# Gated cross-attention kernel: in the transfer queue, queries and keys are written and read back before the probabilities are written

## The reference

```python
def _L1_xattn_ref(hidden_states, cross_attention_states, attention_mask, Wq, Wk, Wv, Wo, q_norm_w, k_norm_w):
    q = (hidden_states @ Wq.T).reshape(bsz, q_len, H, HD).transpose(0, 2, 1, 3)
    k = (cross_attention_states @ Wk.T).reshape(bsz, kv_len, KVH, HD).transpose(0, 2, 1, 3)
    v = (cross_attention_states @ Wv.T).reshape(bsz, kv_len, KVH, HD).transpose(0, 2, 1, 3)
    q = _rmsnorm(q, q_norm_w)
    k = _rmsnorm(jnp.repeat(k, GROUPS, axis=1), k_norm_w)
    scores = jnp.einsum('bhqd,bhkd->bhqk', q, k) * scale + attention_mask[:, :, :, :kv_len]
    probs = jax.nn.softmax(scores.astype(jnp.float32), axis=-1).astype(q.dtype)
    out = jnp.einsum('bhqk,bhkd->bhqd', probs, v)
    return out.transpose(0, 2, 1, 3).reshape(bsz, q_len, H * HD) @ Wo.T
...
x = x + jnp.tanh(g_xattn[0]) * _L0_xattn_ref(_layernorm(x), ctx, ctx)
x = x + jnp.tanh(g_ffn[0]) * _L0_ffn_ref(_layernorm(x), ...)
x = x + jnp.tanh(g_xattn[1]) * _L1_xattn_ref(_layernorm(x), ctx, mask, ...)
x = x + jnp.tanh(g_ffn[1]) * _L1_ffn_ref(_layernorm(x), ...)
```

## Time and profile before

| | |
|---|---|
| runs, median of 3 | 743.99 us (740.37 to 744.77) |
| profiled execution, its own time | 738.72 us |
| its span in the trace | 736.9 us |
| PE busy | 712.1 us (97%) |
| DVE busy | 566.4 us (77%) |
| ACT busy | 377.6 us (51%) |
| POOL busy | 371.8 us (50%) |
| mean granted clock of TensorE | 0.995 |
| DMA | 110.31 MB, mean 150 GB/s |

### The profile page before, as it was taken

The page is one execution under the profiler, slowest core; times in us unless marked ns, Lnnn a source line. Parts: engine busy times, 40 slices in busy tenths (PEclk is TensorE's granted clock), DMA queues, the critical chain, the costliest instruction groups (busy, mean ns, idle before and its releaser), DMA issues.

```text
span 736.9 us, 12666 instructions
## 1 busy us (share of the span) xinstructions
PE 712.1 (97%) x3684; PEld 573.4 (78%) x3684; DVE 566.4 (77%) x1171; ACT 377.6 (51%) x1094; POOL 371.8 (50%) x429
## 2 busy tenths in 40 slices
PE   8899999988999999999999999999999999998996
PEld 5455556577888888888888888888888888887774
DVE  4888887566788777777877787787778787778784
ACT  5567664355555545544564545465545654454220
POOL 2568866556444634553564346345625642265331
PEclk9999999999999999999999999999999999999999
DMA  8400104145765675666657665756665666446221
GB/s 307 144 29 30 43 16 158 42 132 147 228 172 156 180 218 141 180 194 182 167 162 215 161 174 143 235 148 186 194 179 149 167 188 200 119 124 161 67 90 63
DMA packets 109283, 110.31 MB, mean 150 GB/s; under 512 B 12576, under 2 KB 78240, under 8 KB 108960
## 3 DMA queue, kind: packets, MB, share of 16 engines
q1 hardware_dynamic: 109216, 109.51, 52.6%
HBM read 69.62 MB, written 39.85 MB: 149 GB/s over the span
## 4 chain that ended last, share of the span: by engine, by line
PE 30%; POOL 21%; issue 16%; DMA 13%; DVE 11%; ACT 5%; SPq 4%; DVEq 0%; ACTq 0%; POOLq 0%
DMA pTf<-p_scratch 7%; POOL qkr L617 6%; POOL wo_lo L604 6%; PE pair L959 5%; PE pair L961 5%; PE pair L960 5%; DMA p_scratch<-p_blocks 4%; DVE qkn L1434 4%; SPq L458 3%; PE pair L999 3%; POOL wq_lo L596 2%; POOL prob L609 2%; PE pair L973 2%; POOL wkv_lo L586 2%; DVE p_blocks L1409 1%
## 5 line engine op out<-in xcount | busy, mean ns | idle before, releaser
L805 ACT ACTIVATE prob<-score,nmax 128x128 f32<-128x128 f32 x256 | 99.8, 391 | 147.8 <-DVE nmax L1399 147.8
L609 POOL TENSOR_TENSOR prob<-prob,erec 128x512 f32<-128x512 f32 x64 | 66.7, 1042 | 123.0 <-DVE erec L1419 123.0
L959 PE MATMUL pair<-wo_hi,oT_hi 128*128 128x512 f32 x256 | 107.3, 419 | 1.2 <-POOL wo_lo L604 1.2
L959 PE MATMUL pair<-wq_hi,nT_hi 128*128 128x512 f32 x256 | 101.7, 397 | 1.3 <-DVE qkn L1434 1.3
L960 PE MATMUL pair<-wo_lo,oT_hi 128*128 128x512 f32 x256 | 100.1, 391 | 0.0
L960 PE MATMUL pair<-wq_lo,nT_hi 128*128 128x512 f32 x256 | 100.0, 391 | 0.0
L961 PE MATMUL pair<-wo_hi,oT_lo 128*128 128x512 f32 x256 | 100.0, 391 | 0.0
L961 PE MATMUL pair<-wq_hi,nT_lo 128*128 128x512 f32 x256 | 100.0, 390 | 0.0
L1424 DVE TENSOR_REDUCE qkss<-qksq 128x5 f32<-128x640 f32 x64 | 52.4, 819 | 48.5 <-ACT qksq L812 48.2
L617 POOL TENSOR_TENSOR qkr<-qkse,neghalf 128x5 f32<-128x5 f32 x64 | 76.7, 1198 | 5.3
L812 ACT ACTIVATE qksq<-pair 128x640 f32<-128x640 f32 x64 | 45.0, 703 | 65.7 <-PE pair L961 65.7
(11 more groups left out here) (171 smaller groups left out, 1700.8 us busy)
## 6 DMA issues: line engine op xcount, KB each, us to landing
qk_scratch<-qk_blocks SPq DMA_DIRECT2D x256, 80.0 KB, 1.9
qkT<-qk_scratch SPq DMA_DIRECT2D x64, 320.0 KB, 3.0
p_scratch<-p_blocks SPq DMA_DIRECT2D x256, 64.0 KB, 1.8
pTf<-p_scratch SPq DMA_DIRECT2D x64, 256.0 KB, 3.4
wq_raw<-in_wq SPq DMA_DIRECT2D x32, 256.0 KB, 4.1
wo_raw<-in_wo SPq DMA_DIRECT2D x32, 256.0 KB, 4.8
wkv_raw<-in_wkv SPq DMA_DIRECT2D x8, 512.0 KB, 4.9
ctxn<-in_ctx_n SPq DMA_DIRECT2D x8, 256.0 KB, 3.3
```

Of the source, the lines that this page charges most:

```text
L609: pool.tensor_tensor(prob[:], prob[:], erec[:].unsqueeze(2).broadcast_to([P, BL, P]), ALU.mult).then_inc(normed, 1)
L805: t = act.activation(prob[:, i, :], score[:, i, :], ACT.Exp, bias=nmax[:, i:i + 1], accum_out=esum[:, i:i + 1])
L959: pe.matmul(out, l_hi, r_hi, start=start, stop=False)
```

## The change

In SP's loop the read of queries and keys of tile n+1 is issued directly behind their writes, in every slot, ahead of the writes of the probabilities of n-1; before, that was so in slots 0 and 1 alone. Nothing else differs.

```diff
                     if on(n + 1):
                         write_qk(n + 1)
-                    if n < 2 and on(n + 1):
                         read_qk(n + 1)
                     if on(n - 1):
                         write_probs(n - 1)
-                    if n >= 2 and on(n + 1):
-                        read_qk(n + 1)
-                    if on(n - 1):
                         read_probs(n - 1)
```

## The result

The change makes the kernel slower: 807.22 us median (804.05 to 808.54, 4 runs) against 743.98 (740.37 to 744.77, 4 runs), a ratio of 1.085 with a 95% interval of 1.081 to 1.090. The forecast was 748, and 740 to 759 as its range. The profiled execution's span is 805.7 us against 736.9. Its busy times hardly differ: DVE 564.2 us, ACT 374.9, POOL 371.3. PE's reads 729.2 us against 712.1, for the same 3684 products, with ends that are modelled.

What follows compares the result with a forecast made beforehand. TensorE was taken to bound the loop at 8.47 us a slot; +5.6 us behind weight loads and -1.6 at the end gave +4.0 on the median 743.99, so 748 us, range 740 to 759.

Steps and rivals of the forecast that it cites:

- TensorE bounds the loop before, and an edit to SP can only cost there: Attention loop: TensorE waits 1.2 us in 440, slots take 8.47 us, so an SP edit gains nothing there.
- A clean slot: Slot without weight loads: probabilities' read 2.2 us later, tile 1.2 us later, absorbed by ACT's 1.93 us idle; no cost.
- L: Landing time in an SP slot, from first write of queries and keys to their read-back; 3.17 us bare.
- L behind the four loads, taken at 4.5: Worst slot: landing between 3.17 and 5.51 us, about 1.0 less without 256 KB of probabilities; ACT's margin 0.3 us.
- L behind the other loads, taken at 3.9: Next slots, with one weight load each: landing assumed between 3.17 and 4.5 us.
- 3.78 for the probabilities' landing in every slot: Probabilities' first write to their read, from SP slot 1: 3.78 us, 0.56 more than the old order's 3.22.
- The lag, taken at 0.8 us a group: TensorE's loss behind weight loads in seven groups of eight slots: 5.6 us in all, bounds 0 and 16.
- the 2.3 us that I gave for landings of 5.51 and then 4.5: TensorE's loss a group behind weight loads if landings stayed as long as today's: about 2.3 us.
- Case 2, SP becomes the bound: Rival: SP's cycle in loading slots 9.17 us against 8.47, lag 18 us in all, about 760 us; chance 0.26.
- Lp: Time in an SP slot from the probabilities' first write to their read; the forecast used 3.78 us.
- The end of the loop: Last slots: earlier read-back shortens ACT's 3.90 us wait for keys; -1.6 us, bounds -1.0 and -3.2.
- The rule of the Trainium skill: SP queue: fixed transfer cost some 2 us, mostly last write's receipt, speaking against two waits in a row; sum unchanged.

Runs made afterwards that it cites:

- quiet_slots: Kernel before with the new order in SP slots with b = 0 and 1 alone (16 of 64): 742.71 us, ratio 1.001.
- the control: Kernel before with weight loads inside the loop cut to 16 columns of each row: 740.08 us, ratio 1.000.
- one_slot: Kernel before with the new order in SP slots with b = 5 alone (8 of 64), behind the four wo loads: 747.16 us, ratio 1.007.
- three_slots: Kernel before with the new order in SP slots with b = 5, 6 and 7 (24 of 64): 767.00 us, ratio 1.035.
- loaded_slots: Kernel before with the new order in SP slots with b = 2 to 7 (48 of 64): 794.87 us, ratio 1.071.
- tail_only: Kernel before with the new order in SP slots 61 and up alone (and 0 and 1, as before): 737.37 us, ratio 0.995.
- small_reads: Changed kernel with 16-column weight loads and, from tile 2 on, reads of a quarter of the columns: 744.54 us, ratio 1.004.
- wait_only: Kernel before with SP waiting for the queries' and keys' landing before writing probabilities, read left in place: 800.75 us, ratio 1.081.
- small_loads: Changed kernel with each weight load inside the loop cut to 16 columns of each row: 777.99 us, ratio 1.050.
- late_probs: Changed kernel with the probabilities' high half behind ACT's squares and low half behind DVE's maxima: 798.13 us, ratio 1.075.
- the four sets: Kernel before with the new order in b = 0, 1; b = 2 to 7; b = 5; or b = 5, 6, 7: 742.71, 794.87, 747.16, 767.00 us.

## Why the prediction was wrong

- **TensorE bounds the loop before, and an edit to SP can only cost there**: right. Quiet slots and the control lie within 0.2% of the kernel before, and no version gained in the loop.
- **A clean slot, 7.34 us from first write to last read, costs nothing**: right for a slot that SP enters in time (quiet_slots). The change's own slots are rarely so: behind a slot that ended late the new writes start directly behind a read of 256 KB, and L was 3.7 to 3.95 even without a load (b = 0), not 3.17.
- **L behind the four loads, taken at 4.5**: this step failed. It measured 5.25 in the slot shown and 5.55 in the mean of b = 5, for 5.6 in the mean before. I had subtracted 1.0 for the 256 KB of probabilities that no longer share the rings. Those stood behind the writes in question, not ahead, and their going brought nothing. This alone decides the worst slot: with 4.5 ACT has the tile at 407.1, within the limit of 407.4; with the 5.57 that one_slot has for L it is 408.2, 0.7 us late, and one_slot lost 5.7 us in its eight such slots, 0.7 each.
- **L behind the other loads, taken at 3.9**: too low for some. Behind the 512 KB load it was 5.05 in the mean, behind single loads of 256 KB 3.9 to 4.3, with a single case above 5.5.
- **3.78 for the probabilities' landing in every slot**: it came from one slot of the prologue. The mean is 4.00, up to 5.48, so 0.22 more, and it is paid in every slot. The last section shows what the long ones have in common.
- **The lag, taken at 0.8 us a group**: this sum failed, in two steps. It followed three slots from the wo load on, started SP in time before them, and named the three loads ahead without working them out. The run that has just these three slots is three_slots, and it lost 25.6 us, 3.2 a group, so that even the part that was worked out was too small by a factor of four: I had cycles of 9.4, 8.8 and 8.4 us, and they were 10.63, 9.56 and 9.12. (That the 5.7 us of one_slot come near my 5.6 is chance, as by my sum that slot alone costs nothing.) The part left out is as large: the slots b = 2 to 4 add 27.7 us (loaded_slots). Six slots in a row load, and SP's cycle in the slots b = 1 to 6 is 8.9 to 11.2 us against 8.47. Also, the 2.3 us that I gave for landings of 5.51 and then 4.5 come to 2.6 by the same steps.
- **Case 2, SP becomes the bound**, had chance 0.26, and is what happened. Its turning point, a mean L of 3.8 in the loaded slots, was passed clearly. Its size, 18 us, was a quarter of the truth for two reasons: it let SP make up 0.8 us in the slots without loads, which with cycles of 9.1 and 10.1 us (b = 7 and 0) it never did (at b = 7 the landings were long, and behind b = 0 the next tile came late, as the probabilities had held up ACT), and it had L at 4.2 with Lp at 3.78, where behind loads L was 4.5 in the mean. By the measured means SP's cycle is 9.84 us, which over 63 slots is 72 us above 8.69, where 68.3 were measured.
- **The end of the loop**: right in kind, and larger alone (-3.5 for -1.6). In the changed kernel little of it is seen: its last two score products span 21.5 us with the one before them, against 22.0 before and 20.4 in tail_only. Behind the last one all three take 41.0 us.
- **The rule of the Trainium skill** ("DMA: Bandwidth & Descriptors", "Anatomy of one DMA", a section on transfers that GpSimd issues) that the fixed cost of a transfer is mostly the receipt of the last write, and that the sequencer does the waiting, spoke against the change, and rightly. But small_reads shows that the fixed part alone is not what hurt: with it and few bytes, the time is 744.5 us.

Shown: the wait and not the read makes nearly all of the cost (wait_only); bytes and not fixed times make it too long (small_loads, small_reads); SP's cycle is the bound (late_probs, the waits); the lag adds up (the four sets). Why single landings take 5 us where their neighbours take 3.2 to 3.6 with the same bytes is not tested by a run; what the traces show of it stands in the last section.

## What to carry to other kernels

In a queue that runs in order, put a read-back behind whatever other work is ready, so that the landing it waits for passes under that work's issue; two landing waits in a row are two full latencies a slot. Judge such a queue by its cycle in the slots that load most and follow the lag over the whole period, from the state that the period itself leaves, not from an idle start. A landing time that was read in a quiet place is a lower bound. Here only the last slots, where ACT waited for the read-back, gained by an earlier read.

## What the hardware showed that was not expected

A read of 320 KB with the writes of the probabilities right behind it lands as a rule in 3.0 to 3.1 us, but now and then in over 5. In tail_only one was issued at 683.40 and ACT had its data at 688.76. The DMA lines of 683 to 690 (40 slices of 0.175 us: mean busy share in tenths, then GB/s) show no crowding in the last part:

```profile
DMA  0000000792577998667740101001861000000000
GB/s 0 0 0 0 0 0 0 59 102 73 161 234 293 380 407 302 179 173 196 202 120 23 15 0 15 15 0 41 214 158 32 21 21 23 9 0 0 0 0 0
```

From about 686.7 on at most 23 GB/s move for a microsecond. The burst behind it is mostly the last of the probabilities' four writes, as these took 3.20 us to issue in place of 1.8. What goes on meanwhile is in the list of DMA queues of that stretch (685 to 688: transfers, MB, share of 16 engines' time):

```profile
q8 instruction: 1, 0.02, 3.1%
```

This is a transfer of 16 KB that brings instructions; 3.1% of 16 engines over 3 us is 1.5 us of one engine. Such transfers are in every run, and they go with the long landings. Here is one in small_reads, where little else is in the way: writes of queries and keys that took 4.99 us to land (SP's timeline; then the queues of 234 to 239):

```profile
234.08 1.83 SPq L458 DMA_DIRECT2D qk_scratch<-qk_blocks  x4
239.07 0.34 SPq L472 DMA_DIRECT2D qkT<-qk_scratch  x1
```

```profile
q8 instruction: 1, 0.02, 2.2%
```

Of this version's 96 landings (L and Lp of the same 48 slots) 12 took over 4.3 us, and an instruction transfer of 16 KB ran during each of the 12; of the other 84 that holds for 6. (One of 6.10 us behind these slots has none; it stands behind a load of feed-forward weights that this version leaves whole.) The mean landing is 4.42 us with such a transfer and 3.25 without. In the changed kernel 29 of 96 took over 4.3 us. An instruction transfer of 8 or 16 KB ran during 21 of them, and during 15 of the 67 shorter ones; the other 8 of the 29 all stand behind the 512 KB load or the four loads of wo. All 36 of its landings with such a transfer took 0.64 us more than the others in the mean; by estimate (36 x 0.64 / 48) that is 0.5 us a slot of SP's 9.84. The kernel before has the same transfers; there the landings mostly pass under other work. No run left them out, so that this is a coincidence that was counted, and no cause that was tested.
